# Macaron block with attention: the softmax sum is divided out of the head sums on Pool, no longer out of the probabilities on VectorE

## The chip, the cores and the metric

The kernel runs on one core of one Trainium2 chip. Its engines are TensorE (PE, with its weight loads, PEld), VectorE (DVE), ScalarE (ACT), GpSimd (Pool) and SyncE (SP), which here only issues DMAs. The metric is the time of one execution on the device in microseconds; each kernel is timed in several runs and the median is given.

## The reference

The input x is 4 x 1024 tokens of 1024 numbers, in float32. Three residual steps follow one another:

```python
x = x + 0.5 * ffn(layernorm(x))
x = x + attn(layernorm(x))
x = x + 0.5 * ffn(layernorm(x))
```

`ffn` is a dense product with a 1024x1024 weight and a bias, kept only for tokens and output columns whose cluster was hit. What matters here is `attn`: it attends within one token, across the 32 places of each head, not across tokens:

```python
q = einsum('bse,edh->bsdh', x, Wq) + bq          # 32 heads of 32
k, v = ...                                       # 8 heads of 32, repeated 4 times
scores = einsum('bsdh,bseh->bsde', q, k) / sqrt(32)
attn = softmax(scores, axis=-1)
out = einsum('bsde,bseh->bsdh', attn, v)
```

So each token has 32 rows (d) of 32 scores (e). Each row has its own sum, and the output of each row d is that row's probabilities against v, for all heads.

## The kernel before

The 4096 tokens are 32 tiles (NT) of 128 tokens. The kernel has three stages: the first `ffn` (up to about 400 us), a loop that holds the attention and, in its gaps, half of the last `ffn` (about 400 to 1030 us), and the rest of the last `ffn`. Every engine has its own program, written out by hand, and the engines meet only by semaphores: the order of the lines of one engine is the order in which its work runs.

The attention loop has a counter i that every engine runs through in the same way, and a tile passes it in a pipeline: in step i, tile i is layer-normed, tile i-1 is projected to q, k and v, tile i-2 has its scores, softmax and head products, tile i-3 has its head sums stored and loaded again, and tile i-4 gets them added (x2), is layer-normed a third time, and feeds a product of the last `ffn`.

The attention of a tile is done in another order than that of the tokens. q, k and v are stored to HBM and loaded again as blocks (L540 to L556, L517 to L524, all issued by SP), so that a partition no longer stands for a token. ScalarE spreads q over a block-diagonal tile, q_diag (L888), and PE makes the scores with it and k_diag (L1406). DVE then takes the row maxima and subtracts them (L1115, L1120), turns v (L1125), waits for ScalarE's exponential (L902), sums each row (L1127), takes the reciprocals (L1129), adds the bias to the q and k of the next tile (L1134), multiplies the 128x1024 probabilities by the reciprocals (L1139), computes the low half of the third layer norm's split (L1090), turns the probabilities in 32x32 blocks (L1148) and adds the bias to v (L1153). PE makes the head products with the turned probabilities (L1451). ScalarE copies them to o_head (L878) and stores them; SP loads them back as o_tok, 128 tokens by 256, in token order (L531). In the next step DVE adds o_tok to the tile, four times repeated (L1083, in add_heads), and takes the layer norm's statistics. Pool turns the statistics into the factors of the layer norms (L309 to L314), multiplies the first `ffn`'s result by its mask (L678) and adds it to x (L684, in add_first).

The semaphore prob_step counts three steps for each tile on DVE: the sum, the reciprocals and the multiplication. It has one reader on another engine, add_first on Pool:

```python
wait(pool, prob_step, 3 * (t - 2))
```

so Pool's addition for one tile starts only when the multiplication of an earlier one is over. `ones` is a 128x128 tile that is the moving operand of two small matmuls (L367), one ahead of the attention and one behind it.

Of the kernel before, what the change touches and what calls it, by code (L numbers as in the profile page):

```python
# [13 lines left out]
P = 128  # L14
# [20 lines left out]
def macaron_kernel(nc, x_in, Wq, bq, Wk, bk, Wv, bv, W, ffn_bias, centroids, assignments, out):  # L35
# [23 lines left out]
    with ExitStack() as ctx:  # L59
        def sb(name, shape, dt=F32):  # L60
            return ctx.enter_context(nc.sbuf_tensor(name, shape, dt))

        def sem(name):
            return ctx.enter_context(nc.semaphore(name))
# [6 lines left out]
        cen = sb("cen", [P, KB, 2 * NCL], F32R)  # L71
        odd_hi, odd_lo = sb("odd_hi", [P, KB, 2, P], F32R), sb("odd_lo", [P, KB, 2, P], F32R)
        ident = sb("ident", [P, P])
        ones = sb("ones", [P, P])
        own_t = sb("own_t", [P, T4])
        minus_half = sb("minus_half", [P, 1])
        minus_one = sb("minus_one", [P, 1])
# [18 lines left out]
        minus_mean = [sb(f"minus_mean{n}", [P, 1]) for n in range(2)]  # L96
        row_max = sb("row_max", [P, HEADS])
        row_sum = sb("row_sum", [P, HEADS])
        row_inv = sb("row_inv", [P, HEADS])


        with ExitStack() as first:
# [85 lines left out]
        def wait(eng, semaphore, value):  # L188
            if value > 0:
                eng.wait_ge(semaphore, value)  # L190
# [28 lines left out]
        q_ready, v_ready = sem("q_ready"), sem("v_ready")  # L219
        scores, soft_max, scores_read, exp_done = sem("scores"), sem("soft_max"), sem("scores_read"), sem("exp_done")  # L220
        prob_step, probs_ready, heads = sem("prob_step"), sem("probs_ready"), sem("heads")
        o_ready, o_stored, o_in = sem("o_ready"), sem("o_stored"), sem("o_in")
        x2, x2_stored = sem("x2"), sem("x2_stored")
        stats3, var3, power3, norm3 = sem("stats3"), sem("var3"), sem("power3"), sem("norm3")
        y3, t3, hi3, lo3 = sem("y3"), sem("t3"), sem("hi3"), sem("lo3")
# [138 lines left out]

        def select_count(pe, n):
            pe.wait_ge(m_hit, 2 * n + 2)
            pe.matmul(ps_s[0:NCL, 0:P], hit[:, :], ones[:, :], start=True, stop=True).then_inc(m_count, 1)  # L367

        def select_on(dve, n):
            dve.wait_ge(m_count, n + 1)  # L370
# [12 lines left out]
        with nc.Block() as block:  # L383
# [228 lines left out]
            def _(pool):  # L612
# [67 lines left out]
                def add_first(t):  # L680
# [3 lines left out]
                    pool.tensor_tensor(x_ring[t % RING][:, :], x_ring[t % RING][:, :], f_tmp[:, :],  # L684
                                       ALU.add).then_inc(x1, 1)

                mask_first(0)
                add_first(0)
                for i in range(0, NT + 3):
                    if 0 <= i - 4 < NT - 1:  # L690
                        layer_norm_factors(pool, 1, i - 4, var3, power3, norm3, 2)
                    if i < NT:
                        layer_norm_factors(pool, 0, i, var2, power2, norm2, 1)
                    if i == 0:
                        mask_first(1)
                        add_first(1)
                        select_tokens(NT - 3)
                    if i == 1:
                        pool.wait_ge(on_set, NP)
                        pool.wait_ge(f1_read[0], NT - 1)  # L700
                        pool.tensor_scalar(f_out[0][:, half(0)], f_out[0][:, half(0)], token_on[0][:, NT - 2:NT - 1], None,
                                           ALU.mult).then_inc(f1_on, 1)
                    if 2 <= i < 5:
                        t, h = TAIL_HALVES[i - 2]
                        pool.wait_ge(f1_read[h], t + 1)
                        for c in range(2):
                            last = pool.tensor_scalar(f3_out[c][:, :], f3_out[c][:, :], token_on[0][:, t:t + 1], None,
                                                      ALU.mult)
                        last.then_inc(f1_on, 1)
                    if 0 < i and i + 1 < NT:  # L710
                        mask_first(i + 1)
                        add_first(i + 1)
                layer_norm_factors(pool, 1, LAST, var3, power3, norm3, 2)


# [238 lines left out]
            def _(dve):  # L954
# [120 lines left out]
                    dve.tensor_tensor(lo, ps_t[:, :, :], hi.bitcast(F32), ALU.subtract).then_inc(lol, 1)  # L1075

                def add_heads(t):
                    dve.wait_ge(o_in, 16 * (t + 1))
                    dve.wait_ge(y2, t + 1)
                    x2_v = x_ring[t % RING][:, :].rearrange("p (d g r) -> p d g r", g=HKV, r=SCALE)  # L1080
                    o_v = o_tok[:, :].rearrange("p (g d) -> p d g", g=HKV)
                    o_v = o_v.unsqueeze(3).to_broadcast([P, D, HKV, SCALE])
                    dve.tensor_tensor(x2_v, x2_v, o_v, ALU.add).then_inc(x2, 1)  # L1083
                    dve.wait_ge(x2, t + 1)
                    layer_norm_stats(dve, x_ring[t % RING], 1, t, stats3, var3, norm3)
# [6 lines left out]
                for i in range(0, NT + 3):  # L1092
# [19 lines left out]
                    if 0 <= i - 2 < NT:  # L1112
# [11 lines left out]
                            dve.wait_ge(f1_stored[1], 16 * (NP - 1))  # L1124
                        dve.transpose(v_diag[:, :], v_pad[:, :]).then_inc(v_ready, 1)  # L1125
                        dve.wait_ge(exp_done, t + 1)
                        dve.reduce_sum(row_sum[:, :], probs_v, AX.X).then_inc(prob_step, 1)  # L1127
                        dve.wait_ge(prob_step, 3 * t + 1)
                        dve.reciprocal(row_inv[:, :], row_sum[:, :]).then_inc(prob_step, 1)  # L1129
                    if 0 <= i - 1 < NT:  # L1130
                        t = i - 1
                        dve.wait_ge(proj_qk, t + 1)
# [1 line left out]
                        dve.tensor_tensor(qkv_tok[:, 0:2 * HD], ps_b[:, 0:2 * HD], proj_bias[:, 0:2 * HD],  # L1134
                                          ALU.add).then_inc(qk_read, 1)
                    if 0 <= i - 2 < NT:
                        t = i - 2
                        dve.wait_ge(prob_step, 3 * t + 2)
                        dve.tensor_tensor(probs_v, probs_v, row_inv[:, :].unsqueeze(2).to_broadcast(WIDE),  # L1139
                                          ALU.mult).then_inc(prob_step, 1)  # L1140
                    if i == NT + 2:
                        add_heads(LAST)
                    if 0 <= i - 4 < NT - 1:
                        low_third(i - 4)
                    if 0 <= i - 2 < NT:
                        t = i - 2
                        dve.wait_ge(prob_step, 3 * t + 3)
                        dve.transpose(probs[:, :], probs[:, :]).then_inc(probs_ready, 1)  # L1148
                    if 0 <= i - 1 < NT:
                        t = i - 1  # L1150
                        dve.wait_ge(proj_v, t + 1)
# [351 lines left out]
```

## Time and profile before

| | |
|---|---|
| three runs | 1221.32, 1223.47, 1224.46 us |
| median | 1223.47 us |
| span of the profiled execution, first to last instruction | 1220.6 us |
| PE busy | 1207.2 us, 99% |
| VectorE busy | 858.3 us, 70% |
| ScalarE busy | 412.6 us, 34% |
| Pool busy | 420.5 us, 34% |
| HBM, mean | 171 GB/s |

The profile is of one execution; besides its span it gives no total time for it. The rows further down are of two kinds. A row of a group of instructions has busy time and the mean ns of one, then the time that its engine sat idle just before them and what ended it. A row of the timeline has the start and the duration in us, then the engine, the line of the kernel, the operation, what it writes and reads, and in brackets the idle time before it. Matmuls are pipelined, so the duration of one is longer than the distance between two.

### The profile page before, as it was taken

The page shows a single profiled execution, that of the slowest core. Times are in us where ns is not written, and L with a number is a line of the kernel's source. Part 1 is how long each engine was busy: PE and PEld are TensorE (multiplying, and loading weights), DVE is VectorE, ACT ScalarE, POOL GpSimd, SP SyncE. Part 2 cuts the span into 40 slices and gives each one's busy share as a digit, 9 for nine tenths or more (in the row PEclk, how much of TensorE's full clock was granted, in tenths as well). Part 3 has the DMA queues.
Part 4 walks back from the last instruction along what each step waited for, and adds up shares of the span by engine and source line. Part 5 has one row for each costly group of instructions (what it writes and reads, how often), then busy time and mean ns, then how long its engine had stood idle before and what let it go on. Part 6 is the DMA issues. An engine that isn't in the chain of part 4 may idle for free.

```text
span 1220.6 us, 21763 instructions
## 1 busy us (share of the span) xinstructions
PE 1207.2 (99%) x8536; PEld 1039.3 (85%) x8536; DVE 858.3 (70%) x1272; ACT 412.6 (34%) x590; POOL 420.5 (34%) x551
## 2 busy tenths in 40 slices
PE   7999999999999999999999999999999999999998
PEld 6888888888888888888888888888888888888887
DVE  6644654554463587888878888788888874289897
ACT  5322232222121234444444444444434443212120
POOL 1344445444226443233333333333233200050322
PEclk9999999999999999999999999999999999999999
DMA  8577767775754456555565555555555555117885
GB/s 275 148 198 243 200 196 208 226 205 163 202 135 167 110 132 177 148 153 136 156 164 139 153 151 154 156 140 159 135 169 141 137 151 183 38 54 248 302 288 194
DMA packets 318982, 208.54 MB, mean 171 GB/s; under 512 B 258336, under 2 KB 281632, under 8 KB 318880
## 3 DMA queue, kind: packets, MB, share of 16 engines
q1 hardware_dynamic: 303712, 187.74, 53.5%
q10 hardware_dynamic: 15168, 19.40, 4.7%
q8 instruction: 68, 1.11, 0.4%
q14 instruction: 34, 0.28, 0.1%
HBM read 118.49 MB, written 88.60 MB: 170 GB/s over the span
## 4 chain that ended last, share of the span: by engine, by line
PE 79%; DVE 7%; DMA 7%; issue 3%; SPq 2%; POOL 1%; ACT 1%; POOLq 0%; DVEq 0%; ACTq 0%
PE ps_b L276 12%; PE ps_b L278 12%; PE ps_b L277 12%; PE ps_a L276 9%; PE ps_a L278 9%; PE ps_a L277 9%; PE ps_t L283 5%; PE ps_s L1406 4%; PE ps_s L290 2%; DMA late<-x_scratch 2%; PE ps_s L292 2%; PE ps_s L1451 2%; DMA qkv_scratch<-qkv_tok 1%; DMA y_scratch<-xa 1%; DVE late L1188 1%
## 5 line engine op out<-in xcount | busy, mean ns | idle before, releaser
L276 PE MATMUL ps_a<-w_hi,odd_hi 128*128 128x512 f32 (+1 forms) x472 | 187.6, 397 | 0.0
L278 PE MATMUL ps_a<-w_hi,odd_lo 128*128 128x512 f32 (+1 forms) x472 | 183.5, 389 | 0.0
L277 PE MATMUL ps_a<-w_lo,odd_hi 128*128 128x512 f32 (+1 forms) x472 | 183.0, 388 | 0.0
L276 PE MATMUL ps_b<-proj_hi,y_hi 128*128 128x256 f32 (+1 forms) x512 | 177.7, 347 | 0.0
L278 PE MATMUL ps_b<-proj_hi,y_lo 128*128 128x256 f32 (+1 forms) x512 | 172.7, 337 | 0.0
L277 PE MATMUL ps_b<-proj_lo,y_hi 128*128 128x256 f32 (+1 forms) x512 | 172.0, 336 | 0.0
L309 POOL TENSOR_TENSOR var_eps<-moments,eps 128x1 f32<-128x1 f32 x96 | 18.4, 191 | 394.9 <-DVE moments L305 394.9
L684 POOL TENSOR_TENSOR x_ring<-x_ring,f_tmp 128x1024 f32<-128x1024 f32 x32 | 77.1, 2410 | 156.4 <-DVE probs L1139 112.7
L989 DVE TENSOR_TENSOR f_out<-ps_b,bias_a 128x512 f32<-128x512 f32 x30 | 20.7, 691 | 140.5 <-PE ps_b L278 140.4
L632 POOL TENSOR_SCALAR f_out<-f_out,token_on 128x1024 f32<-128x1024 f32 x30 | 85.6, 2855 | 75.8 <-DVE f_out L989 75.6
L278 PEld LDWEIGHTS ps_b<-proj_hi,y_lo 128*128 128x128 f32 x512 | 97.1, 190 | 10.8
L277 PEld LDWEIGHTS ps_b<-proj_lo,y_hi 128*128 128x128 f32 x512 | 97.3, 190 | 9.4
L276 PEld LDWEIGHTS ps_b<-proj_hi,y_hi 128*128 128x128 f32 x512 | 97.2, 190 | 9.0
L278 PEld LDWEIGHTS ps_a<-w_hi,odd_lo 128*128 128x128 f32 x472 | 88.6, 188 | 18.7
L276 PEld LDWEIGHTS ps_a<-w_hi,odd_hi 128*128 128x128 f32 x472 | 88.7, 188 | 17.2
L277 PEld LDWEIGHTS ps_a<-w_lo,odd_hi 128*128 128x128 f32 x472 | 88.8, 188 | 16.9
L318 ACT ACTIVATE q_diag<-x_ring,norms 128x1024 f32<-128x1024 f32 x64 | 79.6, 1244 | 57.5 <-PE ps_s L1406 40.7
L725 POOL TENSOR_TENSOR late<-late,mask 128x1024 f32<-128x1024 f32 x18 | 43.6, 2435 | 138.9 <-DMA late<-x_scratch 91.9
L1095 DVE TENSOR_TENSOR y_lo<-ps_t,y_hi 128x1024 fp32r<-128x1024 f32 x32 | 39.2, 1224 | 62.9 <-ACT y_hi L871 62.9
L276 PE MATMUL ps_b<-w_hi,odd_hi 128*128 128x512 f32 (+1 forms) x208 | 80.8, 389 | 0.0
L278 PE MATMUL ps_b<-w_hi,odd_lo 128*128 128x512 f32 (+1 forms) x208 | 80.3, 386 | 0.0
L277 PE MATMUL ps_b<-w_lo,odd_hi 128*128 128x512 f32 (+1 forms) x208 | 80.3, 386 | 0.0
(192 smaller groups left out, 2726.1 us busy)
## 6 DMA issues: line engine op xcount, KB each, us to landing
xa<-in_L_attn_x SPq DMA_DIRECT2D x32, 512.0 KB, 5.0
f_tmp<-f_scratch SPq DMA_DIRECT2D x32, 512.0 KB, 4.5
x_ring<-in_L_attn_x SPq DMA_DIRECT2D x32, 512.0 KB, 3.4
f_scratch<-f_out SPq DMA_DIRECT2D x30, 512.0 KB, 3.9
x_scratch<-x_ring SPq DMA_DIRECT2D x30, 512.0 KB, 3.2
y_scratch<-xa SPq DMA_DIRECT2D x28, 512.0 KB, 4.3
ya_tok<-y_scratch SPq DMA_DIRECT2D x112, 128.0 KB, 3.3
late<-x_scratch SPq DMA_DIRECT2D x22, 512.0 KB, 6.9
```

What stands on the lines that cost most here:

```text
L276: pe.matmul(acc, hi[:, k, :], w_h[:, k, cols], start=(k == 0), stop=False)
L277: pe.matmul(acc, hi[:, k, :], w_l[:, k, cols], start=False, stop=False)
L278: last = pe.matmul(acc, lo[:, k, :], w_h[:, k, cols], start=False, stop=(k == KB - 1))
L283: last = pe.transpose(ps_t[:, k, :], src[:, k * P:(k + 1) * P], ident[:, :])
L290: last = pe.matmul(pair_ps, cen[:, k, :], hi[:, k, :, :], start=(k == 0), stop=(k == KB - 1))
L292: pe.matmul(pair_ps[0:NCL, :], cen[:, k, 0:NCL], lo[:, k, :, :], start=False, stop=False)
L318: return act.activation(y, x, ACT.Identity, bias=norms[of][:, t, 0:1], scale=norms[of][:, t, 1:2])
L632: pool.tensor_scalar(f_out[t % 2][:, :], f_out[t % 2][:, :], token_on[0][:, t:t + 1], None, ALU.mult).then_inc(f1_on, 1)
L684: pool.tensor_tensor(x_ring[t % RING][:, :], x_ring[t % RING][:, :], f_tmp[:, :], ALU.add).then_inc(x1, 1)
L725: pool.tensor_tensor(f[:, :], f[:, :], mask[:, :], ALU.mult).then_inc(s_masked, 1)
L1095: dve.tensor_tensor(y2_lo[:, :, :], ps_t[:, :, :], y2_hi[:, :, :].bitcast(F32), ALU.subtract).then_inc(lo2, 1)
L1406: last = pe.matmul(ps_s[:, j * P:(j + 1) * P], q_diag[:, j * P:(j + 1) * P], k_blocks[:, j, :, :], start=True, stop=True)
```

## The change

The probabilities go unnormalized into the head products. The 128x32 sums are written in another order of columns, turned by a DVE transpose into token order (sum_tok), and their reciprocals go to one of three buffers, inv_tok. DVE no longer multiplies the probabilities. Pool multiplies o_tok, 128x256, by inv_tok (scale_heads) when it is loaded, and DVE's add_heads waits for that in place of the load. The transpose of the probabilities now stands ahead of the low half of the third layer norm. The third step of prob_step is now the reciprocal. `ones` shrinks to one column that the two matmuls read as a broadcast.

```diff
-        ones = sb("ones", [P, P])
+        ones = sb("ones", [P, 1])
...
-        row_inv = sb("row_inv", [P, HEADS])
+        sum_tok = sb("sum_tok", [P, D])
+        inv_tok = [sb(f"inv_tok{n}", [P, D]) for n in range(3)]
...
-            pe.matmul(ps_s[0:NCL, 0:P], hit[:, :], ones[:, :], start=True, stop=True).then_inc(m_count, 1)
+            pe.matmul(ps_s[0:NCL, 0:P], hit[:, :], ones[:, :].to_broadcast([P, P]), start=True, stop=True).then_inc(m_count, 1)
...
+                def scale_heads(t):
+                    o_v = o_tok[:, :].rearrange("p (g d) -> p g d", g=HKV)
+                    inv = inv_tok[t % 3][:, :].unsqueeze(1).to_broadcast([P, HKV, D])
+                    pool.wait_ge(o_in, 16 * (t + 1))
+                    pool.wait_ge(prob_step, 3 * (t + 1))
+                    pool.tensor_tensor(o_v, o_v, inv, ALU.mult).then_inc(o_scaled, 1)
+
                 mask_first(0)
                 add_first(0)
                 for i in range(0, NT + 3):
+                    if 0 <= i - 4 < NT - 1:
+                        scale_heads(i - 4)
                     if 0 <= i - 4 < NT - 1:
                         layer_norm_factors(pool, 1, i - 4, var3, power3, norm3, 2)
...
+                scale_heads(LAST)
                 layer_norm_factors(pool, 1, LAST, var3, power3, norm3, 2)
...
                 def add_heads(t):
-                    dve.wait_ge(o_in, 16 * (t + 1))
+                    dve.wait_ge(o_scaled, t + 1)
                     dve.wait_ge(y2, t + 1)
...
                         dve.wait_ge(exp_done, t + 1)
-                        dve.reduce_sum(row_sum[:, :], probs_v, AX.X).then_inc(prob_step, 1)
+                        dve.reduce_sum(row_sum[:, :].rearrange("p (r j) -> p j r", r=R4),
+                                       probs[:, :].rearrange("p (j r e) -> p j r e", r=R4, e=D),
+                                       AX.X).then_inc(prob_step, 1)
                         dve.wait_ge(prob_step, 3 * t + 1)
-                        dve.reciprocal(row_inv[:, :], row_sum[:, :]).then_inc(prob_step, 1)
+                        dve.transpose(sum_tok[:, :], row_sum[:, :]).then_inc(prob_step, 1)
+                        wait(dve, o_scaled, t - 2)
+                        dve.wait_ge(prob_step, 3 * t + 2)
+                        dve.reciprocal(inv_tok[t % 3][:, :], sum_tok[:, :]).then_inc(prob_step, 1)
...
                     if 0 <= i - 2 < NT:
-                        t = i - 2
-                        dve.wait_ge(prob_step, 3 * t + 2)
-                        dve.tensor_tensor(probs_v, probs_v, row_inv[:, :].unsqueeze(2).to_broadcast(WIDE),
-                                          ALU.mult).then_inc(prob_step, 1)
+                        dve.transpose(probs[:, :], probs[:, :]).then_inc(probs_ready, 1)
                     if i == NT + 2:
                         add_heads(LAST)
                     if 0 <= i - 4 < NT - 1:
                         low_third(i - 4)
-                    if 0 <= i - 2 < NT:
-                        t = i - 2
-                        dve.wait_ge(prob_step, 3 * t + 3)
-                        dve.transpose(probs[:, :], probs[:, :]).then_inc(probs_ready, 1)
```

## Rows read from the trace of the kernel before

**Rows 1.** The page, parts 1 and 2: busy us by engine; TensorE's granted clock.
```profile
PE 1207.2 (99%) x8536; PEld 1039.3 (85%) x8536; DVE 858.3 (70%) x1272; ACT 412.6 (34%) x590; POOL 420.5 (34%) x551
...
PEclk9999999999999999999999999999999999999999
```

**Rows 2.** The page, part 4: shares of the chain that ended last.
```profile
PE 79%; DVE 7%; DMA 7%; issue 3%; SPq 2%; POOL 1%; ACT 1%; POOLq 0%; DVEq 0%; ACTq 0%
```

**Rows 3.** Waits, whole span, PE's four longest: us in total, times, longest.
```profile
PE ps_a L1246 <- DMA w_raw<-in_L_ffn_weight: 5.8, 1, 5.8
...
PEld ps_s L1406 <- ACT q_diag L888: 3.3, 3, 2.3
...
PEld ps_s L1451 <- DVE probs L1148: 2.8, 16, 0.2
PEld ps_s L1451 <- issue: 2.7, 16, 0.2
```

**Rows 4.** Busy us of each engine in a stretch of the loop.
```profile
500.00:600.00 100.00, 100.00 (x914) 88.72 (x913) 82.35 (x123) 42.90 (x68) 34.24 (x55) 1.00 0.56 157
```

**Rows 5.** Groups by shape, whole span: busy us, mean ns, idle before.
```profile
L678 POOL TENSOR_TENSOR f_tmp<-f_tmp,mask 128x1024 f32<-128x1024 f32 x32 | 68.8, 2151 | 4.8 <-DMA f_tmp<-f_scratch 4.1 <-ACT mask L381 0.6
...
L1139 DVE TENSOR_TENSOR probs<-probs,row_inv 128x1024 f32<-128x1024 f32 x32 | 38.9, 1215 | 0.0
...
L329 DVE COPY pair_exp_in<-ps_s 128x128 f32<-128x128 f32 x32 | 8.6, 269 | 7.6 <-PE ps_s L297 7.6
...
L349 DVE RECIPROCAL pair_inv<-pair_sum 128x2 f32<-128x2 f32 x32 | 5.3, 166 | 1.1
```

**Rows 6.** Timeline of one loop step: start us, us, engine, line, operation.
```profile
721.10 0.35 DVE L1129 RECIPROCAL row_inv<-row_sum 128x32 f32<-128x32 f32 x1
721.30 0.39 PE L278 MATMUL ps_b<-proj_hi,y_lo 128*128 128x512 f32 x1
...
721.73 0.69 DVE L1134 TENSOR_TENSOR qkv_tok<-ps_b,proj_bias 128x512 f32<-128x512 f32 x1 [0.28 <-PE ps_b L278]
...
723.72 2.41 POOL L684 TENSOR_TENSOR x_ring<-x_ring,f_tmp 128x1024 f32<-128x1024 f32 x1 [4.85 <-DVE probs L1139]
...
724.79 1.23 DVE L1148 STREAM_TRANSPOSE probs<-probs 128x1024 f32<-128x1024 f32 x1
...
726.25 0.76 PE L1451 MATMUL ps_s<-probs,v_diag 128*32 128x32 f32 x64
...
728.54 1.21 DVE L1083 TENSOR_TENSOR x_ring<-x_ring,o_tok 128x1024 f32<-128x1024 f32 x1
...
729.09 1.71 ACT L888 ACTIVATE q_diag<-q_head,own_t 128x256 f32<-128x256 f32 x4 [1.45 <-DMA q_head<-qkv_scratch]
...
732.52 0.72 PE L1406 MATMUL ps_s<-k_diag,q_diag 128*128 128x128 f32 x5
```

**Rows 7.** Timeline: q_diag and scores where they stand closest in the steady steps.
```profile
575.26 1.71 ACT L888 ACTIVATE q_diag<-q_head,own_t 128x256 f32<-128x256 f32 x4 [1.94 <-DMA q_head<-qkv_scratch]
...
578.20 0.49 PE L1406 MATMUL ps_s<-k_diag,q_diag 128*128 128x128 f32 x3
```

**Rows 8.** The chain that ended last in order of time, first loop steps.
```profile
431.81 0.23 issue
432.04 0.64 DVE qkv_tok L1134
...
462.35 2.05 PE ps_s L1406 x16
```

**Rows 9.** Timeline: Pool's addition and DVE's addition of heads overlap.
```profile
454.54 2.41 POOL L684 TENSOR_TENSOR x_ring<-x_ring,f_tmp 128x1024 f32<-128x1024 f32 x1 [7.20 <-DMA x_ring<-in_L_attn_x]
...
456.29 1.74 DVE L1083 TENSOR_TENSOR x_ring<-x_ring,o_tok 128x1024 f32<-128x1024 f32 x1
```

**Rows 10.** Timeline, end of the loop: the last tile's factors and their reader.
```profile
1029.94 0.19 POOL L314 TENSOR_TENSOR norms<-minus_mean,norms 128x1 f32<-128x1 f32 x1
...
1032.93 1.25 ACT L318 ACTIVATE q_diag<-x_ring,norms 128x1024 f32<-128x1024 f32 x1
```

More of the change, by code:

```diff
@@ L221, in macaron_kernel @@
         prob_step, probs_ready, heads = sem("prob_step"), sem("probs_ready"), sem("heads")
-        o_ready, o_stored, o_in = sem("o_ready"), sem("o_stored"), sem("o_in")
+        o_ready, o_stored, o_in, o_scaled = sem("o_ready"), sem("o_stored"), sem("o_in"), sem("o_scaled")
         x2, x2_stored = sem("x2"), sem("x2_stored")
```

## The prediction

> **What bounds the kernel now.** I read the page's first two parts first. TensorE (PE) is busy for 1207.2 of 1220.6 us, VectorE (DVE) for 858.3 and Pool for 420.5, and the granted clock of TensorE stands at full speed, 2.4 GHz, in all 40 slices, so no clock is there to be won or lost [rows 1]. A busy PE need not be PE at its peak, since the ends of matmuls are modelled, so the busy share alone proves little. The chain of work that ended last says the same by another road: 79% of it is PE and 7% DVE [rows 2]. The third view is the one that decides: what PE and its weight loads waited for, over the whole span [rows 3]. There PE waits 5.8 us for the first weights, before any attention work exists; its weight loads wait 3.3 us in three places for q_diag ahead of the scores; and 2.8 us for the turned probabilities ahead of the head products, as 16 waits of at most 0.2 us. The attention loop, where the change sits, has nothing else. A stretch out of its middle has PE busy for 100 of 100 us and DVE for 82 [rows 4]. So DVE is loaded, but it is not what PE waits for. Taking work from it can give back at most the waits in those rows: 3.3 + 2.8 = 6.1 us, 0.5% of the time.
>
> **What leaves DVE.** 32 multiplications of 128x1024 at 1215 ns go, 38.9 us of DVE time [rows 5]. Follow one loop step in order of time [rows 6]: the reciprocal runs at 721.10, the bias addition L1134 at 721.73 (it sat idle for 0.28 us until PE's last matmul of the projection, begun at 721.30), the multiplication follows and then the low half L1090, and the transpose of the probabilities begins at 724.79 and ends at 726.02. PE starts the head products at 726.25, 0.2 us later. The multiplication's removal and the transpose's new place ahead of L1090 bring the transpose forward by about 2.4 us (two instructions of 1.2 us no longer stand before it). L1090 stays where it is, with a transpose of 1.23 us before it in place of a multiplication of 1.22. What is PE worth of this? The 0.2 us are counted as a wait for the transpose in 16 steps [rows 3]. In the other 16 the waits view puts a gap of the same length to "issue", with the transpose long done; so I take the gap as what it takes PE to start this product anyway and the gain as 0, with 2.8 us as its bound.
>
> **What comes onto DVE.** 32 transposes of 128x32, between the sum and the reciprocal. No row has this shape. The nearest are small instructions: 166 ns for 128x2 and 269 ns for 128x128 [rows 5]; a straight line between these gives about 0.19 us for 32 elements, and I take 0.20. The upper bound is the 1.23 us of the 128x1024 transpose [rows 6]; below 0 it can't be, since an instruction is added on a path that loses none ahead of L1134. Its hand-over costs some 0.03 us, as from the sum to the reciprocal. So 0.23 us, at most 1.26. The reciprocal itself has the same 32 elements (0.35 us [rows 6]), and the sum reads the same elements in the same order and writes 32 results to other places: 0 is taken. DVE's busy time should fall by 38.9 - 32 x 0.20 = 32.5 us, to about 826 us.
>
> What stands behind these 0.23 us? L1134, which frees the projection's accumulator and starts the path store of q and k, load of q_head and k_diag, q_diag on ScalarE, scores on PE. Queued behind it on DVE are the transpose and L1090. In the steady steps 0.28 us of idle time before L1134 takes it in [rows 6]. At the upper bound 1.26 - 0.28 = 0.98 us would be left, and the reserve at the end of that path is next: q_diag ends at 729.09 + 1.71 = 730.80 and the scores start at 732.52, 1.7 us later; in the tightest step that I found it is 578.20 - (575.26 + 1.71) = 1.2 us [rows 7]. So 0 in the steady steps at either end.
>
> The first steps of the loop are another matter. There the chain that ended last does not run through PE but round a loop of DMAs: store of v, load of v_pad, transpose, sum, reciprocal, L1134, store of q and k, and on. The 0.23 us in front of L1134 at 432.04 are that reciprocal's, on the chain, and it comes out at the scores at 462.35, where PE has been waiting for q_diag [rows 8]. The added 0.23 us lie right in it: +0.2 us once. At the upper bound it is 1.3 us, and with a second turn round that loop 2.5 us.
>
> **What comes onto Pool.** 32 multiplications of 128x256, two inputs in SBUF. The multiplication of 128x1024 on Pool takes 2151 ns [rows 5]; scaled by length over a start of 0.19 us (Pool's 128x1 instructions, as in [rows 10]) this is about 0.68 us; bounds 0.5 us (a quarter of the row) and 2.15 us (the row itself, if the shape with its broadcast gains nothing). It sits between Pool's add_first and the addition of heads on DVE, L1083, which now waits for Pool instead of for the DMA; queued behind L1083 are both layer-norm statistics and the next softmax. In the steady step add_first ends at 723.72 + 2.41 = 726.13 and L1083 starts at 728.54 [rows 6], so Pool has 2.4 us for it: hidden, even at 2.15. The o_tok load that Pool waits for is issued in the step before, and Pool's own queue is free by then. Add_first moves too: its wait for the third step of prob_step was for the multiplication's end and is now for the reciprocal, some 2 us earlier, so the reserve grows to more than 4 us where this wait ends last. What was behind it then is the load of x_ring, or nothing.
>
> At the loop's end there is no add_first; the last o_tok load is followed by Pool's 0.68 us, the last L1083 and its statistics and factors. The factors ended at 1029.94 + 0.19 = 1030.13, and ScalarE used them only at 1032.93 [rows 10]: 2.8 us of reserve against 0.7 (2.15 at most) plus about 0.6 us if the product queues behind the factors of the tile before. Hidden. The matmul with `ones` broadcast happens twice, both times alone between products: 0. Nothing is changed at SP's queue or in any transfer.
>
> **Two rules against a row.** When Pool's add_first ran from 454.54 to 456.95, a DVE L1083 that started at 456.29 took 1.74 us in place of the usual 1.21, which is as if it had stood still until Pool ended [rows 9]. The Trainium skill (SBUF — State Buffer, "Who interferes with whom") has this as a rule: a DVE instruction with two SBUF inputs and a Pool instruction that reads SBUF shut each other out for the whole instruction. It speaks against a new two-input product on Pool. By it the scale product can delay only L1083 and the small 128x128 steps; in the steady steps Pool is done before L1083, so the sum stays, and if it did hit L1083 each time DVE would lose 0.7 us of its 18 idle per 100. The skill (GPSIMD Engine Reference, "Engine selection") also advises VectorE for elementwise work, with Pool about half as fast; the rows give 2151 against 1215 ns for the same shape, and neither lies on PE's path here.
>
> **The sum.** Span 1220.6 + 0.2 (first steps) + 0 (steady steps, Pool, tail) = 1220.8 us. The page has no other total; the median of the three runs, 1223.47, stands 2.9 us above the span, and I carry that over: 1223.7 us.
>
> **Rivals.** (a) Faster: the waits for q_diag and for the turned probabilities are all real and all go, because DVE is lighter: 1223.5 - 6.1 = 1217.4 us. For it: the 16 waits are named after the transpose that moves. Against it: the same gap is there without it, and the three waits for q_diag hang on the DMA loop, which the change lengthens. 4%. (b) Slower: the path to L1134 grows by more than 0.28 + 1.2 = 1.5 us, because the small transpose costs as much as the large one and the sum, which now writes its results permuted, twice its 1.2 us. Then 1.23 + 1.21 = 2.4 us are added, 0.9 more than the tighter half of the steps can take: 16 x 0.9 + 2 x 2.4 = 19 us, 1243 us. For it: neither form is in the trace. Against it: small DVE instructions all cost 0.17 to 0.35 us. 4%. (c) Slower by Pool: the scale product takes over 2.4 us, L1083 and the statistics slip, and with them the layer norm that PE transposes. At 3.4 us, 1 us in each of some 28 steps, 1252 us at worst. It would need Pool to be five times slower for each element than in its row. 2%. (d) The forecast: DVE's freed time turns into idle time. 90%.
>
> **How the numbers follow.** About 0.3% (3.7 us) is what a measurement of this kernel can tell from no change. The forecast's own bounds are -2.8 us (all 16 waits) and +2.5 us (the DMA loop at the upper bound), so 1220.9 to 1226.2; a little is added for the runs' own spread (1221.3 to 1224.5 before): 1220.5 to 1226.5. Outside are the rivals, about one in ten. Chances: faster 0.04, same 0.89, slower 0.07.
>
> **What would show it.** In the changed kernel's profile: DVE's busy time near 826 us and Pool's near 442, PE's unchanged; the small transpose at 0.2 us; the transpose of the probabilities ending over 2 us before the head products, and PE's gap before them still 0.2 us; the scale product at 0.7 us, over before L1083; the wait for q_diag near 460 us as long as before or a little longer. Wrong would be a new row in PE's waits: for q_diag or k_diag in the steady steps (b), or for the third layer norm (c). Gone waits ahead of the scores near 460 us would speak for (a).

## The result, and the profile after

Before 1223.72 us (median of 4 runs, 1221.32 to 1224.46), after 1234.78 us (4 runs, 1233.28 to 1235.99): a ratio of 1.0093, interval [1.0079, 1.0108]. The change makes the kernel 11 us slower; the forecast was no change. The profiled executions have spans of 1220.6 and 1233.8 us.

The page of after, parts 1, 2 and 4, against [rows 1, 2]:

```profile
PE 1214.4 (98%) x8536; PEld 1039.6 (84%) x8536; DVE 828.3 (67%) x1272; ACT 412.8 (33%) x590; POOL 443.0 (36%) x583
...
PEclk9999999999999999999999999999999999999999
...
PE 76%; DMA 12%; DVE 4%; SPq 4%; issue 2%; ACT 1%; POOL 1%; POOLq 0%; DVEq 0%
```

VectorE has its 30 us less and Pool its 22 us more, as forecast. But TensorE (PE), whose instructions are the same 8536, is busy for 7.2 us more at the same granted clock. That is the first line to stop at: a busy time that grows with no instruction added. In the chain, DMA has gone from 7% to 12%.

What PE waited for in after, against [rows 3]:

```profile
PEld ps_s L1415 <- ACT q_diag L899: 5.5, 4, 3.0
PEld ps_s L1460 <- issue: 5.4, 32, 0.2
...
PE ps_t L284 <- DVE odd_lo L1101: 1.9, 2, 1.2
...
PE ps_s L291 <- DVE odd_lo L1101: 1.1, 2, 0.6
```

The wait for q_diag is 2.2 us longer, and there is a new one for odd_lo, the output of low_third. These are 5 us. But the one for odd_lo is not the change's alone: the kernel before with 32 unused bytes behind its last tile (the control further down) has it too,

```profile
PE ps_s L291 <- DVE odd_lo L1091: 1.0, 1, 1.0
```

and over the other traces here, those of the last three experiments aside, it goes from none to 2.6 us in all. So the 3 us here can't be charged to the moved work. The rest is in no wait. Two stretches of the first stage show it, where nothing of the changed work runs (the columns are those of [rows 4]; x is the number of matmuls). Before:

```profile
100.00:200.00 100.00, 100.00 (x477) 83.75 (x476) 53.34 (x107) 27.98 (x37) 48.91 (x59) 1.00 0.74 210
200.00:300.00 100.00, 100.00 (x479) 83.88 (x478) 52.87 (x101) 29.05 (x37) 46.93 (x58) 1.00 0.70 198
```

After:

```profile
100.00:200.00 100.00, 100.00 (x471) 82.92 (x471) 52.13 (x106) 29.13 (x38) 49.90 (x57) 1.00 0.75 205
200.00:300.00 100.00, 100.00 (x472) 82.92 (x472) 52.27 (x104) 26.95 (x36) 47.11 (x59) 1.00 0.74 203
```

PE is busy for 100 of 100 us in all four, at a granted clock of 1.00, and gets through 6 or 7 matmuls fewer. The timeline of PE shows where. Before, one product of the first stage:

```profile
187.00 0.39 PE L276 MATMUL ps_b<-w_hi,even_hi 128*128 128x512 f32 x1
187.22 0.39 PE L277 MATMUL ps_b<-w_lo,even_hi 128*128 128x512 f32 x1
187.45 0.39 PE L278 MATMUL ps_b<-w_hi,even_lo 128*128 128x512 f32 x1
187.68 0.39 PE L276 MATMUL ps_b<-w_hi,even_hi 128*128 128x512 f32 x1
```

After:

```profile
187.10 0.40 PE L277 MATMUL ps_b<-w_hi,even_hi 128*128 128x512 f32 x1
187.34 0.39 PE L278 MATMUL ps_b<-w_lo,even_hi 128*128 128x512 f32 x1
187.57 0.39 PE L279 MATMUL ps_b<-w_hi,even_lo 128*128 128x512 f32 x1
187.80 0.40 PE L277 MATMUL ps_b<-w_hi,even_hi 128*128 128x512 f32 x1
```

Three matmuls take 0.68 us before and 0.70 after. Over the matmuls of 512 columns the mean distance from one start to the next, by the tiles read, is as follows (distances over 0.3 us, some 4% of them, have a wait or another product's start in them and are left out). In each, even, odd or y is the weights, which PE has loaded, and w or proj is the moving tile:

| product | matmuls | before | after |
|---|---|---|---|
| w_hi with even | 496 | 0.2278 us | 0.2339 us |
| w_lo with even | 248 | 0.2276 | 0.2321 |
| w_hi with y (last stage) | 192 | 0.2277 | 0.2320 |
| w_lo with y (last stage) | 96 | 0.2268 | 0.2358 |
| w_hi with odd | 1328 | 0.2281 | 0.2279 |
| proj with y | 768 | 0.2286 | 0.2285 |

By this table 496 x 6.1 + 248 x 4.5 + 192 x 4.3 + 96 x 9.0 ns = 5.8 us come from products that the change doesn't touch, and those with odd and proj are as fast as before.

The other part is in DMAs. The trace's list of DMA issues (KB each, median us from issue to landing) has these for the load of ya_tok in the first stage and for the store of q and k in the loop, before:

```profile
ya_tok<-y_scratch SPq DMA_DIRECT2D x112, 128.0 KB, 3.3
...
qkv_scratch<-qkv_tok SPq DMA_DIRECT2D x32, 256.0 KB, 3.0
```

After:

```profile
ya_tok<-y_scratch SPq DMA_DIRECT2D x112, 128.0 KB, 3.8
...
qkv_scratch<-qkv_tok SPq DMA_DIRECT2D x32, 256.0 KB, 3.2
```

From the issue of the store to SP's next issue the median is 2.98 us before and 3.24 after. Same bytes, same issue, 9% longer. By the kernel's access patterns both of these transfers go in pieces of 32 numbers, 128 bytes; the load of x_ring, in whole rows of 4 KB, has 3.4 us in both traces.

Setting the n-th matmul of one trace beside the n-th of the other, the 13.3 us between them arise so: 4.8 in the first stage, 7.1 in the attention loop (6.3 of it as eight late starts of 0.5 to 1.3 us: scores at 407, 442, 462 and 887 us of before, behind odd_lo at 628, 648, 880 and 898), 1.4 behind the loop.

**Theory P, Q and W.** What in the diff can reach the steady products of the first stage? Only the tiles' places in SBUF. `ones` shrinks from 512 to 4 bytes a partition (32 with padding), which is -480, and three inv_tok and sum_tok replace row_inv, which is +384: all tiles behind both move by -96 bytes. The compiled kernels place them so (start in bytes in the partition; w and odd stand ahead of `ones`):

| tile | before | after |
|---|---|---|
| w_hi, odd_hi | 16512, 86144 | 16512, 86144 |
| proj_hi | 116352 | 116256 |
| even_hi, and y2_hi in the same place | 165504 | 165408 |
| even_lo, and qkv_tok in the same place | 173696 | 173600 |

Before, all start at a multiple of 128. After, those of the last three rows start 32 bytes behind a multiple of 64. P says that placement is the cause; Q, its sharper form, that a matmul is slow when its weights and its moving tile start at different places modulo 64. W, the rival, says that the moved work is the cause, and R, beside P, that this work has 0.3 to 0.5% of its own.

### The profile page after: what moved, and what is told of

Its sections match the earlier page's. It is cut to its first block, busy times and chain, and to the rows that moved or that the text cites. A ratio compares the mean times of both kernels' runs of the same rounds, so it can differ in the third digit from the quotient of the medians.

```text
span 1233.8 us, 21856 instructions
## 1 busy us (share of the span) xinstructions
PE 1214.4 (98%) x8536; PEld 1039.6 (84%) x8536; DVE 828.3 (67%) x1272; ACT 412.8 (33%) x590; POOL 443.0 (36%) x583
## 3 DMA queue, kind: packets, MB, share of 16 engines
q8 instruction: 68, 1.11, 0.4%
## 4 chain that ended last, share of the span: by engine, by line
PE 76%; DMA 12%; DVE 4%; SPq 4%; issue 2%; ACT 1%; POOL 1%; POOLq 0%; DVEq 0%
PE ps_b L277 12%; PE ps_b L279 12%; PE ps_b L278 12%; PE ps_a L277 9%; PE ps_a L279 9%; PE ps_a L278 9%; DMA qkv_scratch<-qkv_tok 6%; PE ps_t L284 4%; PE ps_s L1415 4%; PE ps_s L291 2%; PE ps_s L293 2%; DMA v_pad<-qkv_scratch 2%; SPq L551 1%; PE ps_s L1460 1%; SPq L523 1%
## 5 line engine op out<-in xcount | busy, mean ns | idle before, releaser
L1106 DVE TENSOR_TENSOR y_lo<-ps_t,y_hi 128x1024 fp32r<-128x1024 f32 x32 | 39.2, 1225 | 77.9 <-ACT y_hi L882 77.9
```

Of the source, the lines that this page charges most:

```text
L1106: dve.tensor_tensor(y2_lo[:, :, :], ps_t[:, :, :], y2_hi[:, :, :].bitcast(F32), ALU.subtract).then_inc(lo2, 1)
```

## The experiments

Interval in brackets, always against the kernel before on the same chip. "+32" is a tile of 32 bytes that nothing uses.

**The kernel before with the small `ones` alone.**

```diff
-        ones = sb("ones", [P, P])
+        ones = sb("ones", [P, 1])
...
-hit[:, :], ones[:, :],
+hit[:, :], ones[:, :].to_broadcast([P, P]),
```

> The kernel before with one part of the change alone: ones is one column, read as a broadcast. All that comes behind it in SBUF moves down by 480 bytes, so every large tile starts at 32 mod 64 bytes in place of 0 mod 64. Theory P (placement: the starts at 32 mod 64 slow PE's operand reads and the DMAs): 1232 to 1236 us, as the changed kernel. Rival W (the work that moved between VectorE and Pool makes the loss): 1223.7 us, as before, since no such work moves here.

Measured 1234.63 us, 1.0076 [1.0054, 1.0099]. No attention work is changed and four fifths of the loss are there. W falls as the main cause. even_hi starts at 165024, again 32 behind a multiple of 64.

**Which tiles.** Two kernels before, the first with +32 ahead of and behind even and y2, the second with +32 behind them only:

```diff
+            sa("pad_a", [P, 8])
             even_hi, even_lo = ...
+            sa("pad_b", [P, 8])
...
+            sb2("pad_c", [P, 8])
             y2_hi, y2_lo = ...
+            sb2("pad_d", [P, 8])
```

> The kernel before with only even_hi, even_lo, y2_hi and y2_lo (what PE loads as weights) moved to 32 mod 64, everything behind them at 0 mod 64. Theory P, in parts: the drift of 6.4 us in the two product stages comes back and the loop's waits stay as before: 1229 to 1231 us. If the starts matter only to the DMAs, 1223.7. Rival W: 1223.7 us.

Measured 1235.03 us, 1.0080 [1.0051, 1.0109]: 4 us over the range that I expected.

> The kernel before with PE's weights left where they are and only the tiles behind them (qkv_tok, q_head, o_head, o_tok, the token tiles and the diagonals) moved to 32 mod 64. Theory P, in parts: the DMAs of the loop take 0.25 us longer each, the waits for q_diag in the first steps grow as in the changed kernel (some 2 us) with up to 4 us in later steps: 1226 to 1230 us; PE's products keep their pace. Rival W: 1223.7 us.

Measured 1229.60 us, 1.0039 [1.0020, 1.0058]. In the first, even is at 32 modulo 64 and qkv_tok, with all that lies behind it, at 64 modulo 128; I had counted 0 modulo 64 as unmoved, and it isn't: the store of q and k takes 3.24 us in both kernels. In the second even is where it was and qkv_tok at 32. Between the two lie 0.4% for the matmul tiles, though the two intervals touch. PE's own times are clearer, 1217.9 us busy against 1209.7 (the page, part 1). The first:

```profile
PE 1217.9 (99%) x8536; PEld 1041.9 (84%) x8536; DVE 858.2 (70%) x1272; ACT 412.7 (33%) x590; POOL 421.6 (34%) x551
```

The second:

```profile
PE 1209.7 (99%) x8536; PEld 1042.5 (85%) x8536; DVE 857.2 (70%) x1272; ACT 412.8 (34%) x590; POOL 421.7 (34%) x551
```

In the first, proj (at 0) with y (at 32) has become slow as well, 0.2329 us, where after has 0.2285 with both at 32. That speaks for Q, and is the other part of the miss: I had counted on even and y alone. Its products of 256 columns are not slower by it (0.121 us from start to start against 0.123 in the kernel before).

**The changed kernel, +32.**

```diff
+        sb("pad", [P, 8])
         with ExitStack() as first:
```

> The changed kernel with an unused tile of 32 bytes behind the small tiles, so that every large tile starts at 0 mod 64 again; nothing else is altered. Theory P: 1223 to 1225 us, so the work that moved is worth nothing either way. Rival W: 1234.8 us, as the changed kernel.

Measured 1230.92 us, 1.0049 [1.0032, 1.0066]: neither the 1223 to 1225 us of P nor the 1234.8 of W. The large tiles from proj on start at multiples of 64, but of 128 no more: w with even takes 0.2296 us (0.2339 in after), the store of q and k still 3.24 us. P with "modulo 64" was too coarse.

**Everything at 32 modulo 64, w and odd too.**

```diff
+        sb("pad", [P, 8])
         w_hi, w_lo = sb("w_hi", [P, KB, EMB], F32R), ...
```

> The kernel before with 32 unused bytes ahead of w_hi: every tile, w_hi and w_lo too, starts at 32 mod 64. Theory Q (what counts is whether the weights and the moving operand of a matmul start at different places mod 64, since the one is loaded while the other streams): all are alike again, so PE's products stay at 0.227 to 0.229 us and the time is that of before, ratio 1.000 to 1.003. Rival: a start at 32 mod 64 is slow by itself: ratio 1.010 or more, with all products at 0.232 us and over.

Measured 1.0024 [1.0012, 1.0037]. Its timeline of PE:

```profile
187.63 0.39 PE L277 MATMUL ps_b<-w_hi,even_hi 128*128 128x512 f32 x1
187.85 0.39 PE L278 MATMUL ps_b<-w_lo,even_hi 128*128 128x512 f32 x1
188.08 0.39 PE L279 MATMUL ps_b<-w_hi,even_lo 128*128 128x512 f32 x1
188.31 0.39 PE L277 MATMUL ps_b<-w_hi,even_hi 128*128 128x512 f32 x1
```

0.68 us again, with even at the same 32 modulo 64 as in after. So it isn't the place of a tile but the difference of the two; Q is shown for the products of 512 columns. Those of 128 don't follow it: the transposes with ident at 0 and q_diag at 32 modulo 64 keep 0.109 us in after. What is left, 0.24%, goes with the two DMAs: 3.24 us for the store of q and k here too, and 3.9 for the load of ya_tok. Where it arises can be seen matmul by matmul. Between 395 and 480 us, the first loop steps with their loop of DMAs, PE falls behind the kernel before by 3.1 us in this trace and by 3.0 in the second kernel of "Which tiles"; in the five versions of the kernel before further down whose large tiles start at the old places it is -0.3 to 0.6. That other transfers of the moved tiles have a part in it is not excluded.

**The changed kernel with the large tiles exactly where they were (+96), and a control.**

```diff
+        sb("pad", [P, 24])
         with ExitStack() as first:
```

> The changed kernel with 96 unused bytes behind the small tiles: every large tile has exactly the address it has in the kernel before; the small ones stay at 32 mod 64. Theory P (placement is all): ratio 1.000 to 1.002, and PE's products with even_hi and y_hi back from 0.232 to 0.228 us. Rival R (a rest of 0.3 to 0.5% belongs to the work that moved, through the DMA loop of the first steps and the waits in later ones): ratio 1.003 to 1.005, as the version with 32 bytes, with the extra in waits ahead of the scores.

Measured 1226.94 us, 1.0019 [1.0002, 1.0037]: R's 0.3% and more is out. On another chip, once more:

> The changed kernel plus 96 bytes ahead of the large tiles, a second time (an equal kernel gave 1.0019 [1.0002, 1.0037] on another chip). If the rest of about 0.2% belongs to the moved work: 1.0015 to 1.0025. If it was that chip's or those runs' own: under 1.0010. It is the base for the other three runs here.

Measured 1227.71 us, 1.0018 [1.0004, 1.0031]. All products are back at 0.2269 to 0.2286 us, the store at 2.98 us. So of the 0.93% some 0.74 (9 us) are placement, and 0.19 stay with the moved work. The control, the kernel before with +32 behind everything:

> The kernel before with 32 unused bytes behind its last tile, so that no tile moves. A control: what a run of the same work differs by on this chip, and what its trace shows in the waits. Every theory: ratio 1.000, PE's products at 0.227 to 0.230 us from one to the next.

Measured 0.9998 [0.9983, 1.0012]. And a changed kernel with its small tiles at multiples of 64 too (+32 behind `ones`, +64 ahead of the large tiles):

> As the version with 96 bytes, but the small tiles too start at 0 mod 64, as before. If the small tiles' starts matter (the bias tile that VectorE reads, the sums), this one is faster than the version with 96 bytes by what they cost; theory P with them: ratio 1.000. Rival R: 1.003 to 1.005, and the same as the version with 96 bytes.

Measured 1.0024 [1.0011, 1.0036]: the small tiles have no part that can be measured.

**The rest of 0.2%.** Theory S: it is the small transpose ahead of L1134, on the DMA loop of [rows 8]. First the kernel before with that transpose into a tile that nothing reads, between sum and reciprocal; then the changed kernel (+96) with small transpose and reciprocal moved behind the transpose of the probabilities, and Pool's wait moved to the sum; then the kernel before with L1134 ahead of the reciprocal:

```diff
+                        dve.transpose(spare[:, :], row_sum[:, :]).then_inc(turned, 1)
+                        dve.wait_ge(turned, t + 1)
                         dve.reciprocal(row_inv[:, :], row_sum[:, :]).then_inc(prob_step, 1)
```

> The kernel before, every tile where it was, with one instruction more: VectorE turns the 128x32 sums into a spare tile that nobody reads, and the reciprocal waits for that, as in the changed kernel. Theory S (the rest of 0.2% that stays when the tiles are placed as before is the 0.25 us that the small transpose adds ahead of L1134): ratio 1.001 to 1.003, with the extra in waits for q_diag in the first steps and for odd_lo in later ones. Rival: the rest comes from Pool's product or from the new order: ratio 1.000.

Measured 1.0003 [0.9988, 1.0019].

> The changed kernel with the large tiles placed as before (96 unused bytes), and the small transpose and the reciprocal moved behind the transpose of the probabilities, so that L1134 follows the sum at once; Pool's add_first waits for the sum in their place. Theory S: 0.6 us leave the path store of q and k, q_diag, scores, so the waits for q_diag in the first steps shrink below those of the kernel before: ratio 0.998 to 1.000. Rival: ratio 1.002, as the version with 96 bytes, if the rest is not on that path.

Measured 1.0019 [1.0006, 1.0031].

> The kernel before with the reciprocal moved behind L1134, nothing else: 0.35 us leave the same path. Theory S: 0.9985 to 1.000. It tells whether what the version with the late sum gains belongs to the order alone or also to the multiplication that VectorE no longer makes: if both give the same ratio, the change itself is worth nothing even when it is placed well.

Measured 1.0006 [0.9991, 1.0021]. All three speak against S: alone the transpose costs at most 0.19% by its interval, and 0.03% is the best guess; taken off that path it gives nothing back. Pool's part alone, o_tok multiplied by ones in the kernel before:

```diff
+                    pool.tensor_tensor(o_v, o_v, one, ALU.mult).then_inc(o_scaled, 1)
...
-                    dve.wait_ge(o_in, 16 * (t + 1))
+                    dve.wait_ge(o_scaled, t + 1)
```

> The kernel before, every tile where it was, with Pool's product alone: Pool multiplies o_tok by ones (the 128x256 shape of the change) and add_heads waits for it; VectorE's work is as before. Theory S: ratio 1.000. Rival: Pool's product and the wait for it make the rest: ratio 1.002 or more.

Measured 1.0006 [0.9989, 1.0023]. Both parts together in the kernel before:

> The kernel before with both added parts at once, none of their use: a small transpose of the sums between sum and reciprocals on VectorE, and Pool's product of the loaded head sums by ones. Alone they gave 1.0003 and 1.0006. If the rest is the sum of the two additions: 1.0009 to 1.0020. If it is in what the change takes away or reorders: 1.0000 to 1.0009.

Measured 1.0016 [0.9996, 1.0035]. And the changed kernel (+96) with low_third ahead of the transpose of the probabilities again, where theory T puts the 0.2% on that order:

> As the run before, and the low half of the third layer norm's split (low_third) stands ahead of the transpose of the probabilities again, as in the kernel before. Theory T (the rest is the turned order of these two: PE's second product waits for odd_lo in steps in which v_pad lands late): the new waits for odd_lo go and the ratio is under 1.0008. Rival U (the rest lies in the first stage and outside the span, where this order isn't used): 1.0015 to 1.0025 as without it.

Measured 1.0012 [0.9994, 1.0030], between T and its rival. The run with both parts fits a rest that is the sum of two small additions, and has waits like after's (waits of PE, the same columns as above):

```profile
PE ps_s L292 <- DVE odd_lo L1101: 2.0, 4, 0.9
```

Here low_third has its old order, so the order isn't needed for these waits. Nor do they tell much: the second run of the changed kernel with +96 has none of them and the same 1.0018. All the intervals overlap, and the cause of the 0.2% is not settled.

**Is VectorE's freed time idle time?** The changed kernel (+96) with the multiplication kept (by ones) ahead of the transpose:

```diff
+                        dve.tensor_tensor(probs_v, probs_v, ones[:, 0:1].unsqueeze(2).to_broadcast(WIDE),
+                                          ALU.mult).then_inc(kept, 1)
+                        dve.wait_ge(kept, i - 1)
                         dve.transpose(probs[:, :], probs[:, :]).then_inc(probs_ready, 1)
```

> As the first run, and VectorE keeps its product over the 128x1024 probabilities (by ones, so the values stay), ahead of the transpose. It is the change with its gain taken out: VectorE's busy time 39 us higher. If VectorE's load counts at all the ratio is above the first run's by over 0.1%; if the freed time was idle time anyway, as the prediction has it, the two ratios agree within 0.1%.

Measured 1321.27 us, 1.0780 [1.0754, 1.0806], where I expected 1.002. One step of its timeline:

```profile
769.03 0.35 DVE L1147 RECIPROCAL inv_tok<-sum_tok 128x32 f32<-128x32 f32 x1
...
769.55 2.42 POOL L687 TENSOR_TENSOR x_ring<-x_ring,f_tmp 128x1024 f32<-128x1024 f32 x1 [3.17 <-DVE inv_tok L1147]
769.95 3.10 DVE L1155 TENSOR_TENSOR probs<-probs,ones 128x1024 f32<-128x1024 f32 x1
...
771.91 1.72 POOL L695 TENSOR_TENSOR o_tok<-o_tok,inv_tok 128x256 f32<-128x256 f32 x1
...
774.25 1.19 DVE L1103 TENSOR_TENSOR odd_lo<-ps_t,odd_hi 128x1024 fp32r<-128x1024 f32 x1
```

The multiplication takes 3.10 us in place of 1.22: it ends at 773.05, 1.08 us after Pool's addition (771.97). Pool's own product, begun at 771.91, takes 1.72 in place of 0.73 and ends 0.6 us after the multiplication. The two engines take turns. The Trainium skill (SBUF — State Buffer, "Who interferes with whom") has this lock for a DVE instruction with two SBUF inputs against a Pool instruction that reads SBUF; these rows agree. In the changed kernel itself the addition starts as early in the steps where it waits for the reciprocal, and there a transpose with one input runs beside it in its usual 1.23 us. Not all of the 94 us between this trace and that of the changed kernel with +96 are waits: PE waits 64.6 us for odd_lo, and is busy for 1239.3 us against 1209.9. A stretch of the loop (the columns of [rows 4]) shows what goes with it:

```profile
700.00:800.00 100.00, 87.65 (x755) 77.13 (x753) 78.15 (x101) 35.91 (x54) 36.88 (x46) 0.95 0.47 124
```

PE idles for 12 of 100 us, and its granted clock is 0.95 there, where it is 1.00 in every other kernel here. So about a third of the loss is matmuls that themselves take longer, at the lower clock, and not waits. Two runs part the effects. First, Pool's addition waits for the kept multiplication (`wait(pool, kept, t - 2)`), as it did before:

> As the run with the multiplication kept (1.078), but Pool's add_first waits for that multiplication's end, as in the kernel before, in place of the reciprocal's. Theory V (the 96 us came from the two running at the same time: VectorE's product of 2.8 to 3.1 us in place of 1.2): it goes back to 1.2 us, and the ratio to 1.0010 to 1.0030, as without the multiplication, because the freed time of VectorE is idle time in the changed kernel. Rival (VectorE's 1.2 us in each step cannot be carried any more with the small transpose in front of them, PE waits for odd_lo): 1.005 to 1.08.

Measured 1249.14 us, 1.0195 [1.0175, 1.0215], at a granted clock of 1.00 again. Groups by line on VectorE (busy, mean ns), and PE's waits:

```profile
L1155 DVE TENSOR_TENSOR probs<-probs,ones 128x1024 f32<-128x1024 f32 x32 | 38.8, 1213 | 0.0
```

```profile
PE ps_t L286 <- DVE odd_lo L1103: 10.3, 15, 1.2
...
PE ps_s L293 <- DVE odd_lo L1103: 8.7, 14, 1.1
```

The multiplication is back at 1213 ns, and still 1.8% stay, of which 19 us are PE's waits for odd_lo. V was right on the lock and wrong on the rest; its rival came true. low_third has a multiplication and a transpose in front of it here, where before it had the multiplication alone; that is 1.2 us more, and it does not have them to spare. So what VectorE gives up is idle time only as long as nothing is put in its place ahead of low_third. (That it is this order and nothing else which makes the waits is argued; no run keeps the multiplication with low_third in its old place.) Second, the kernel before with Pool's wait one step earlier:

```diff
-                    wait(pool, prob_step, 3 * (t - 2))
+                    wait(pool, prob_step, 3 * (t - 2) - 1)
```

> The kernel before with one number changed: Pool's add_first waits for the reciprocals of the earlier tile in place of its multiplication. Theory V: Pool's addition and VectorE's multiplication start within half a microsecond of each other, the multiplication takes some 3 us in place of 1.215, low_third and the turned probabilities come 1.5 to 2 us later, and the time grows by 3 to 8%. If the two do not disturb one another: 1.000.

Measured 1250.76 us (two runs), 1.0205 [1.0178, 1.0233], under the 3 to 8% expected:

```profile
L1139 DVE TENSOR_TENSOR probs<-probs,row_inv 128x1024 f32<-128x1024 f32 x32 | 73.5, 2298 | 0.0
```

```profile
PE ps_t L283 <- DVE odd_lo L1090: 11.5, 12, 1.1
...
PE ps_s L290 <- DVE odd_lo L1090: 7.9, 7, 1.5
```

One number of a wait is worth 25 us: the multiplication goes from 1215 ns [rows 5] to 2298 on average, though in 13 steps the addition is held back by a later load instead of the reciprocals (Pool's waits). The third step of prob_step in the kernel before keeps the two apart.

No version here is faster than the kernel before. The changed ones with the large tiles at their old places are 0.12 to 0.24% slower; the lowest of these, with low_third in its old order, can't be told from no change.

## Why the prediction was wrong, point by point

- **What bounds the kernel: right, and too narrow.** PE does bound it. From "the attention loop has nothing else" I concluded that only waits could move the time. But a PE that is busy for 100 of 100 us can still get slower: its products are the largest term of all, and I set it at "unchanged".
- **The failed step: `ones` at 0.** I costed its two matmuls ("alone between products: 0") and not its 480 bytes. As an edit of a tile's size it moves the start of every tile behind it. The runs put 9 of the 11 us there: 0.4 to 0.5% by weights and moving tile at different starts modulo 64 (0.2277 to about 0.233 us for each matmul, 5.8 us in the table), and 0.2 to 0.4% with the starts of the tiles that DMAs read and write.
- **"Nothing is changed in any transfer": wrong.** The store of q and k went from 2.98 to 3.24 us, the load of ya_tok from 3.3 to 3.8. The loop of DMAs in the first steps was read rightly [rows 8] and hit as I said, only by more than the 0.2 us of the small transpose: the gaps ahead of the scores grew from 0.37 to 1.11 us and from 2.03 to 2.74.
- **What leaves VectorE: right.** 828.3 us against 826 forecast. The transpose came forward, PE's gap ahead of the head products stayed at 0.2 us (32 times `issue`), and no gain came of it. Rival (a) is dead.
- **The small transpose: right.** The groups by shape of after:

```profile
L1142 DVE STREAM_TRANSPOSE sum_tok<-row_sum 128x32 f32<-128x32 f32 x32 | 6.8, 211 | 1.1
...
L693 POOL TENSOR_TENSOR o_tok<-o_tok,inv_tok 128x256 f32<-128x256 f32 x32 | 23.7, 740 | 16.4 <-DMA o_tok<-o_scratch 16.4
...
L1094 DVE TENSOR_TENSOR x_ring<-x_ring,o_tok 128x1024 f32<-128x1024 f32 x32 | 39.0, 1218 | 2.9 <-POOL o_tok L693 2.9
```

  211 ns against 200 forecast, and in the kernel before it costs nothing that can be measured (1.0003). The sum is no slower for its permuted output (1199 ns). Rival (b) is dead.
- **Pool: right.** 740 ns against 680, busy 443.0 against 442. The addition of heads, now L1094, waited for it twice, 2.9 us in all. Rival (c) is dead, and alone Pool's part gave 1.0006.
- **Steady steps at 0: not upset by these runs, but for a thinner reason than I gave.** In four steps of after PE starts 0.6 to 1.3 us late behind odd_lo; since the control has such a wait too, and one trace of the changed kernel (+96) has none, they show how little there is to spare and not what the change costs. One of them, where v_pad's load lands late:

```profile
883.58 1.25 DVE L1136 STREAM_TRANSPOSE v_diag<-v_pad 128x1024 f32<-128x1024 f32 x1 [1.89 <-DMA v_pad<-qkv_scratch]
...
887.09 1.23 DVE L1153 STREAM_TRANSPOSE probs<-probs 128x1024 f32<-128x1024 f32 x1
...
888.25 1.18 DVE L1101 TENSOR_TENSOR odd_lo<-ps_t,odd_hi 128x1024 fp32r<-128x1024 f32 x1
...
889.58 1.06 PE L284 MATMUL ps_t<-ident,q_diag 128*128 128x128 f32 x8 [1.17 <-DVE odd_lo L1101]
```

  odd_hi was ready at 886.6 (not shown), so low_third stood only behind VectorE's own queue. I had looked for the reserve of L1134's path (1.2 us) and never for low_third's, which the guarded run shows to be under 1.2 us in most steps.
- **The lock between VectorE and Pool: named, and looked for in one place only.** I asked what the new Pool product could hit. I said of add_first's earlier start that "the reserve grows", and did not see that its old wait kept it off the multiplication. That costs nothing here, since the multiplication goes; with it kept it costs 2% and more.
- **The range** was built from the bounds of the named terms. A term without a row can't widen a range, so the placement is what it missed.

## What to carry to other kernels

An edit that changes a tile's size is an edit of all tiles behind it. Before costing such a change, compare the starts of the large tiles in both kernels, and where they move, pad them back: here that is 96 bytes for 9 us. In a trace, compare the number of matmuls in 100 us of a stretch that the change does not touch: with PE 100% busy at the same granted clock in both, and the same order of matmuls, a different count says that the matmuls themselves take longer, and no wait will show it. And a wait that looks as if it only orders data may keep two engines off one another: look at what runs beside its reader before it is moved.

## What the runs showed of the hardware that I had not expected

- A 128x512 matmul whose weights and moving tile start at places that differ by 32 modulo 64 bytes comes every 0.233 us in place of 0.2277, 2.4% later (0.232 to 0.236 by tiles in after); both at 32 is as good as both at 0, and 64 modulo 128 against 0 gave 0.2275 to 0.2300. The rows show no wait for it. Products of 256 columns (0.121 us against 0.123) and transposes of 128 (0.109) were not slower. The Trainium skill (SBUF — State Buffer, "Who interferes with whom") says that only the port pair of VectorE and GpSimd makes contention and that PE waits on no one; that section tells nothing of starts, and the runs show that these matter. What in the chip does it, these runs don't show.
- The store of q and k from SBUF took 2.98 us (median of each trace, up to 2.99) in the 14 traces whose qkv_tok starts at a multiple of 128, and 3.23 to 3.24 us in the six others (starts at 32 or 64), on three chips. The load of ya_tok (median to landing) parts in the same way: 3.3 to 3.4 us against 3.8 to 3.9. Both move 128 bytes at a time, and a load of whole rows (x_ring) didn't part; what makes it so is not shown.
- VectorE's product of 128x1024 with both inputs in SBUF takes up to 3.10 us in place of 1.22 beside a Pool addition of the same size.
